# First linear attention's keys-times-values with values as weights in two column halves; four transferred tiles a head; logarithms and additions on other engines

## The reference

```python
# layer 0, "mix": a performer with 12 heads of 64, M = 384 features
q, k = _feature_map(q, w_orf), _feature_map(k, w_orf)   # exp(x w - |x|^2/2) / sqrt(M)
k_sum = jnp.sum(k, axis=2)
D = jnp.einsum('bhnm,bhm->bhn', q, k_sum)[..., None] + EPSILON
ktv = jnp.einsum('bhnm,bhnc->bhmc', k, v)
out = jnp.einsum('bhnm,bhmc->bhnc', q, ktv) / D
h = x + out @ proj_w + proj_b
y = _layernorm(h, ln2_g, ln2_b)
y = jax.nn.gelu(y @ fc1_w + fc1_b) @ fc2_w + fc2_b
# both layers, "gnn": graph attention with 8 heads
e = jax.nn.leaky_relu(a_src[src] + a_dst[dst], NEG_SLOPE)
ex = jnp.exp(e - m[dst])                 # m: largest e of a target
denom = jax.ops.segment_sum(ex, dst)
out = jax.ops.segment_sum(ex / denom[dst] * h[src], dst)
```

## Time and profile before

| quantity | us |
|---|---|
| median of 3 runs (3369.91 to 3375.5) | 3371.8 |
| the profiled execution | 3377.93 |
| its span | 3376.1 |
| PE busy | 2862.6 (85%) |
| DVE busy | 2279.2 (68%) |
| ACT busy | 1450.8 (43%) |
| POOL busy | 612.2 (18%) |

### The profile page before, as it was taken

One profiled execution on the slowest core, in us unless ns is written; L12 is line 12 of the kernel. 1 busy time (PEld: TensorE's weight loads), 2 busy tenths in 40 slices (PEclk: granted clock), 3 DMA queues, 4 the chain that ended last, 5 costly groups with the idle time before them and its releaser, 6 DMA issues. The chain is left out here.

```text
span 3376.1 us, 50914 instructions
## 1 busy us (share of the span) xinstructions
PE 2862.6 (85%) x17896; PEld 2539.2 (75%) x17896; DVE 2279.2 (68%) x4129; ACT 1450.8 (43%) x2440; POOL 612.2 (18%) x460
## 2 busy tenths in 40 slices
PE   4999997867999997798897599868999976998794
PEld 3999995666788997798896233248999976887794
DVE  6575543856851553798664888756797868998775
ACT  5465462222112332465243577621455532554355
POOL 2777782220000000110002310000000014110000
PEclk9999998988999999899999699979999988998897
DMA  8433326694212653976031312244302058864301
GB/s 272 82 47 57 55 15 171 196 231 109 69 46 68 188 168 99 214 143 143 30 76 33 96 39 47 51 146 131 92 26 67 23 147 216 182 138 108 81 16 48
DMA packets 262710, 351.49 MB, mean 104 GB/s; under 512 B 100252, under 2 KB 178589, under 8 KB 262366
## 3 DMA queue, kind: packets, MB, share of 16 engines
q1 hardware_dynamic: 176574, 272.11, 30.0%
q0 software_dynamic: 85920, 76.71, 11.8%
HBM read 266.35 MB, written 81.40 MB: 103 GB/s over the span
## 5 line engine op out<-in xcount | busy, mean ns | idle before, releaser
L213 POOL DMA_INDIRECT adj_d<-edge_val,edge_off x160 | 336.2, 2101 | 108.5 <-DMA adj_d<-edge_val,edge_off 48.1
L3340 DVE TENSOR_TENSOR expert_wgel<-expert_gel,expert_wps 128x417 f32<-128x417 f32 (+1 forms) x384 | 202.5, 584 | 55.3 <-PE expert_wps L3265 53.3
L2251 PE MATMUL gat00att_ops<-gat00att_h,gat00att_p 125*125 x1600 | 191.2, 284 | 46.6 <-ACT gat00att_p L2161 27.4
L2251 PEld LDWEIGHTS gat00att_ops<-gat00att_h,gat00att_p 125*125 125x125 f32 x1600 | 188.2, 197 | 49.7 <-issue 49.7
L2251 PE MATMUL gat10att_ops<-gat10att_h,gat10att_p 125*125 x1600 | 189.5, 283 | 37.5 <-ACT gat10att_p L2161 21.1
L3312 ACT ACTIVATE expert_gel<-expert_hps 128x417 f32<-128x417 f32 (+1 forms) x384 | 192.9, 519 | 56.2 <-DVE expert_wgel L3340 46.3
L2251 PEld LDWEIGHTS gat10att_ops<-gat10att_h,gat10att_p 125*125 125x125 f32 x1600 | 186.4, 198 | 40.7 <-issue 40.6
L737 ACT ACTIVATE xn_room<-perf_wide,perf_lnm 125x384 f32<-125x384 f32 (+2 forms) x228 | 114.2, 621 | 162.5 <-PE perf_wide L623 89.3
L599 PE MATMUL perf_wide<-y_lo,perf_qk_hi 128*128 128x416 f32 (+1 forms) x432 | 155.0, 359 | 21.5 <-DVE perf_qk_lo L783 21.4
L1361 PE MATMUL fc_ps<-y_lo,fc_w_hi 128*128 128x512 f32 (+1 forms) x432 | 155.1, 359 | 20.4 <-DVE fc_w_lo L1403 20.4
L1514 PE MATMUL fc_ops<-fc_w_hi,fc_x_lo 128*125 128x384 f32 x480 | 163.2, 340 | 7.1 <-DVE fc_w_lo L1566 7.1
(11 more groups left out here) (514 smaller groups left out, 8328.4 us busy)
## 6 DMA issues: line engine op xcount, KB each, us to landing
fc_w<-in_L_mix_fc_w SPq DMA_DIRECT2D x96, 384.0 KB
gat00att_e<-logs_d POOLq DMA_DIRECT2D x24, 546.9 KB, 6.9
gat10att_e<-logs_d POOLq DMA_DIRECT2D x24, 546.9 KB, 7.2
adj_d<-edge_zero POOLq DMA_DIRECT2D x22, 546.9 KB, 14.6
gat00proj_adj<-adj_d POOLq DMA_DIRECT2D x20, 546.9 KB, 8.3
edge_keys<-keys_d SPq DMA_DIRECT2D x20, 437.5 KB
gat00att_sh<-shift_d SPq DMA_DIRECT2D x16, 546.9 KB
sh<-shift_d SPq DMA_DIRECT2D x16, 546.9 KB
```

The source lines that it names most:

```text
L213: edges.nc.gpsimd.indirect_dma_start(out=edges.adj_flat[u].rearrange("(n a) -> n a", a=1), out_offset=bass.IndirectOffsetOnAxis(ap=edges.o ...
L2251: ins = pe.matmul(ops[0:TP, u, b, t * w:(t + 1) * w], p[:, s, (t0 + t) * TP:(t0 + t + 1) * TP], h[:, s, bass.ds(hd, 1), :], start=(s == 0 ...
L3340: dve.tensor_tensor(wgel[:, q % W, 0:cn], gel[:, q % 3, 0:cn], wps[:, q % 3, 0:cn], ALU.mult).then_inc(wgel_done, 1)
```

## The change

- LOGGED becomes (1, 3, 5, 7): four tiles a head in place of three get their logarithm by transfer. PE and ACT both go through the tiles in `order`.
- The logarithms are made in fc1 from the stored counts, no longer in gat00proj; there they were three, here four.
- gat00proj stores the mask strips between the stores of h.
- POOL's first clear in the norm stage waits for the third of five loads of x.
- In performer 0 (`folded=True`), k_t_v has v (125 x 64) as weights and kphi (384 columns) as moving operand; the even token tiles go to partitions 0 to 63 of the result, the odd to 64 to 127. DVE sums the keys over tokens, and PE adds the two halves and turns them by six small matmuls. The copy of ktv for the first head stands behind the split of v's weights and one count. Performer 1 is as before.
- proj_stage has no POOL work: DVE adds bias and row, and ACT normalises.

```diff
@@ -39,7 +39,7 @@
 EG = 4
-LOGGED = (1, 4, 7)
+LOGGED = (1, 3, 5, 7)
 PLAIN = tuple(t for t in range(NT) if t not in LOGGED)
@@ -277,7 +277,7 @@
                 pool.wait_ge(zeroed, 1)
-                pool.wait_ge(x_ld[pairs - 1], 32)
+                pool.wait_ge(x_ld[2], 32)
                 edges.clear(pool, edges.adj_flat[0:1])
@@ -457,6 +457,11 @@
         ktv = S.sb("ktv", [128, 2, mb_n, vw])
+        if folded:
+            halves, fold, ones = S.sb("halves", [128, m]), S.sb("fold", [128, HD]), S.sb("ones", [TP, 1])
+            ksum = edges.zero[:, 0:m] if edges is not None else S.sb("ksum", [TP, m])
+            halves_done, halves_kept, ksum_done, fold_set = (S.sem(s) for s in (
+                "halves_done", "halves_kept", "ksum_done", "fold_set"))
         den = S.sb("den", [TP, NT])
@@ -464,6 +469,7 @@
         o_ps = S.ps("o_ps", [128, 2, 512])
+        ktv_out = o_ps[:, 1, 256:256 + mb_n * vw] if folded else ktv_ps[:, 0:mb_n * vw]
         w_ld, w_high, w_split, o_st = S.sem("w_ld"), S.sem("w_high"), S.sem("w_split"), S.sem("o_st")
@@ -615,6 +621,8 @@
                         for n in range(n_k):
+                            if x == 1 and n == n_k - 3:
+                                fold_halves(0)
                             bank = feature_bank(K0[x] + n)
@@ -629,6 +637,8 @@
                                 pe.wait_ge(s_done, g * 6 + 3 + c + 3)
+                            if x == 1 and c == 1:
+                                fold_halves(1)
                             for mb in range(mb_n):
@@ -641,12 +651,33 @@
                         pe.wait_ge(v_done, i * 5 + 5)
+                        if folded:
+                            pe.wait_ge(halves_kept, g * 2 + x + 1)
+                            for t in range(NT):
+                                r = 64 * (t % 2)
+                                ins = pe.matmul(ktv_ps[r:r + 64, 0:m], v[:, t, 2 * u + x, 0:HD], kphi[:, t, :],
+                                                start=(t < 2), stop=(t >= NT - 2), tile_position=(0, r), skip_group_check=True)
+                            ins.then_inc(halves_done, 1)
+                            return
                         pe.wait_ge(ktv_kept, g * 2 + x + 1)
...
                                                 start=(t == 0), stop=(t == NT - 1))
+                        ins.then_inc(ktv_done, 1)
+
+                    def fold_halves(x):
+                        if not folded:
+                            return
+                        pe.wait_ge(ktv_kept, g * 2 + x + 1)
+                        pe.wait_ge(halves_kept, g * 2 + x + 2)
+                        pe.wait_ge(ksum_done, g * 2 + x + 2)
+                        for mb in range(mb_n):
+                            pe.matmul(ktv_out[:, mb * vw:mb * vw + HD], halves[:, mb * 128:(mb + 1) * 128], fold[:],
+                                      start=True, stop=True)
+                            ins = pe.matmul(ktv_out[:, mb * vw + HD:(mb + 1) * vw], ksum[:, mb * 128:(mb + 1) * 128], ones[:],
+                                            start=True, stop=True)
                         ins.then_inc(ktv_done, 1)
@@ -738,7 +771,11 @@
-                        act.wait_ge(ktv_done, g * 2 + x + 1)
+                        if folded:
+                            act.wait_ge(halves_done, g * 2 + x + 1)
+                            act.wait_ge(ksum_done, g * 2 + x + 1)
+                        else:
+                            act.wait_ge(ktv_done, g * 2 + x + 1)
                         for n in range(n_k):
@@ -850,9 +887,22 @@
+                    def sum_keys(x):
+                        if not folded:
+                            return
+                        dve.wait_ge(exp_done, g * units + K0[x] + n_k + 1)
+                        dve.wait_ge(ktv_done, g * 2 + x + 1)
+                        dve.tensor_reduce(ksum[:], kphi[:].rearrange("p t m -> p m t"), AX.X, ALU.add).then_inc(ksum_done, 1)
+
+                    def keep_halves(x):
+                        if not folded:
+                            return
+                        dve.wait_ge(halves_done, g * 2 + x + 2)
+                        dve.tensor_copy(halves[:], ktv_ps[:, 0:m]).then_inc(halves_kept, 1)
+
                     def keep_ktv(x):
                         dve.wait_ge(ktv_done, g * 2 + x + 2)
-                        dve.tensor_copy(ktv[:, x], ktv_ps[:, 0:mb_n * vw].rearrange("p (a b) -> p a b", a=mb_n)
+                        dve.tensor_copy(ktv[:, x], ktv_out.rearrange("p (a b) -> p a b", a=mb_n)
                                         ).then_inc(ktv_kept, 1)
@@ -885,15 +935,22 @@
                         scan.tiles(dve, hd, 0, 0, 2)
-                    keep_ktv(0)
+                    sum_keys(0)
+                    keep_halves(0)
+                    if not folded:
+                        keep_ktv(0)
                     if u == 0 and not (isinstance(i, int) and i == HP // 2 - 1):
...
                     count(1)
+                    if folded:
+                        keep_ktv(0)
+                    sum_keys(1)
                     keep_out(0)
                     count(2)
+                    keep_halves(1)
                     keep_ktv(1)
@@ -1165,6 +1230,11 @@
+                def normalise(t):
+                    act.wait_ge(centred, t + 1)
+                    act.activation(a[:, t, :] if turn else h[:, t, :], h[:, t, :], ACT.Identity, scale=rstd[:, t:t + 1],
+                                   bias=centre[:, t:t + 1]).then_inc(normed, 1)
+
                 def keep_a(t):
```

proj_stage on DVE, fc1, gat00proj and attention (`mask_after` is `{5: (0, 5), 8: (5, 9), 9: (9, 10)}`):

```diff
@@ -1262,25 +1312,25 @@
-                def normalise(t):
-                    if turn:
-                        if t in first_of:
-                            dve.wait_ge(x_ld[first_of[t]], 32)
-                        dve.tensor_tensor(x[:, t, :], x[:, t, :], h[:, t, :], ALU.add).then_inc(sum_ready, 1)
-
+                def scales(t):
                     dve.wait_ge(std_ready, t + 1)
...
                     steps_done.wait()
-                    dst = a[:, t, :] if turn else h[:, t, :]
-                    dve.tensor_scalar(dst, h[:, t, :], mv[:, t, 0:1], rstd[:, t:t + 1],
-                                      ALU.subtract, ALU.mult).then_inc(normed, 1)
-                    if not turn:
+                    dve.scalar_tensor_tensor(out=centre[:, t:t + 1], in0=mv[:, t, 0:1], scalar=-1.0, in1=rstd[:, t:t + 1],
+                                             op0=ALU.mult, op1=ALU.mult).then_inc(centred, 1)
+
+                def total(t):
+                    if t in first_of:
+                        dve.wait_ge(x_ld[first_of[t]], 32)
+                    if turn:
+                        dve.tensor_tensor(x[:, t, :], x[:, t, :], h[:, t, :], ALU.add).then_inc(sum_ready, 1)
+                    else:
+                        steps_done.done(dve.tensor_tensor(x[:, t, :], x[:, t, :], rows[0:TP, 1, :], ALU.add))
                         dve.wait_ge(normed, t + 1)
                         steps_done.done(dve.tensor_tensor(h[:, t, :], h[:, t, :], rows[0:TP, 0, :], ALU.mult))
-                        dve.wait_ge(shifted, t + 1)
                         steps_done.wait()
-                        total = late.tiles[:, t - NT + 2, :] if late is not None and t >= NT - 2 else x[:, t, :]
-                        dve.tensor_tensor(total, x[:, t, :], h[:, t, :], ALU.add).then_inc(sum_ready, 1)
+                        to = late.tiles[:, t - NT + 2, :] if late is not None and t >= NT - 2 else x[:, t, :]
+                        dve.tensor_tensor(to, x[:, t, :], h[:, t, :], ALU.add).then_inc(sum_ready, 1)
@@ -1343,10 +1404,19 @@
                 sp.wait_ge(next_st, 16)
+                sp.wait_ge(log_st, 32 * len(LOGGED))
...
                 scan.load(pool)
+                for n, s in enumerate(LOGGED):
+                    if n:
+                        pool.wait_ge(log_ready, n)
+                        move_rows(pool, logs_d[n - 1], log[:], log_st)
+                    move_rows(pool, counts[:], counts_d[s * TP:(s + 1) * TP, :], counts_ld)
+                pool.wait_ge(log_ready, len(LOGGED))
+                move_rows(pool, logs_d[len(LOGGED) - 1], log[:], log_st)
+                pool.wait_ge(log_st, 32 * len(LOGGED))
@@ -1389,10 +1459,13 @@
                 act.wait_ge(scan.scanned, 8)
-                with act.Fori(SB // 2 - 1, ob_n // 2 - 1) as i:
+                for i in range(SB // 2 - 1, ob_n // 2 - 1):
                     for u in range(2):
...
                         gelu(i * 2 + u + 1, 1 - u)
+                    n = i - SB // 2 + 1
+                    act.wait_ge(at_least_one, n + 1)
+                    act.activation(log[:], log[:], ACT.Ln).then_inc(logged, 1)
                 gelu(ob_n - 1, 1)
@@ -1420,9 +1493,18 @@
                         scan.finish(dve, hd, x)
-                with dve.Fori(SB // 2, ob_n // 2) as i:
-                    for u in range(2):
-                        low(i * 2 + u, u)
+                for i in range(SB // 2, ob_n // 2):
+                    n = i - SB // 2
```

(44 more changed lines are left out.)

94 lines of the change are left out of this document (45 added, 49 removed).

## The result

The changed kernel takes 3363.1 us (median of 13 runs) where the kernel before takes 3375.2 beside it: ratio 0.996, with an interval of 0.9945 to 0.9976. So it is faster by 12 us, not by 38, and lies 1 us above the range given, 3310 to 3362. (The forecast was made from a median of 3371.8 for before, 3.4 us under the one of all 13 runs.) Its profiled execution has a span of 3358.1 us, 18.0 less than that of before.

What follows compares the result with a forecast made beforehand. Read stage by stage, with PE's instructions setting performer 0's length. Gains 11 + 18 + 8.5 + 0 + 1 + 0 = 38.5 us took 3377.9 to 3339.4, or 3333 us against the median; own range 3318 to 3350, overall 3310 to 3362.

Steps and rivals of the forecast that it cites:

- The step that failed: Performer 0: DVE's key sums take 49 us in all; PE waits 1.6 us in two pairs, about 0.6 us a pair.
- the bound of 4.6 us: Performer 0: upper bound for one DVE key sum of 3840 elements, in proportion to 1.22 us for 1024.
- the first rival: Performer 0: column halves don't overlap, so it loses 25 us instead of gaining 11; 3369 us, chance 0.08.
- the loss at the change of mode: Performer 0: skill page's caution that changing tiling mode drains PE; trace leaves at most about 0.2 us, 24 changes.
- The scatter as next limit: Performer 0: POOL's scatter-adds end at 515.1 us, so the stage ends at 519.5, not 513.6; gain 11 us.
- gat00proj's total: gat00proj: 10.5 us from logarithms leaving plus 9.5 from the tail, less 2 for overlap; gain 18 us.
- the bound of 8: proj1: upper bound of the gain from moving POOL's additions to DVE, forecast at 4 us, lower bound -4.
- The earlier clear: Norm stage: first clear of the adjacency starts some 7 us earlier; gain 1 us, between -1.5 and 4.
- zero was forecast: Both attention stages: fourth transfer's 0.3 us a head offset by 2.4 us a stage at the start; bounds 10 either way.
- the second rival: Attention: accumulates run one behind another, 29.2 us a head for 25.15, 65 us lost; 3398 us, chance 0.08.
- The Trainium skill's formula: Attention: one transfer costs 2.0 us plus bytes at 436 GB/s, 3.3 us for 547 KB; 22 us more gain.
- DVE's new 23.7 a head: Attention: DVE's time per head in us with four transfers, set beside 24.1 us of DMA.

Runs made afterwards that it cites:

- The first run without the fold: Changed kernel with performer 0 as before (30 matmuls a head, no key sum on DVE), all other parts kept: ratio 0.9898, 3345.6 us.
- the short sum: Changed kernel with performer 0's key sum over two of ten token tiles, so denominators are not the reference's: ratio 0.9861, performer 0 471 us.
- the last reordering: Kernel with three transferred tiles and nine additions per key sum, DVE's sum moved ahead of query/key weight split and first count: ratio 0.983, 3322.6 us.
- the two runs on order and number: Performer 0 as before: three transferred tiles with PE in ACT's order, attention 0 234.8 us; four with PE from 0 to 9, 243.1 us.

## Why the prediction was wrong

**The step that failed** is the sum on DVE and what it does to PE: "12 x 4.1 = 49 us on an engine with 262 of 469 us busy", and behind it "PE comes to the fold early: I estimate 1.6 us there, and about 0.6 us a pair". The sum is 6.8 us, 81 in all. It was scaled from a reduction of 1024 neighbouring elements to one of 3840 in another shape, and the bound of 4.6 us taken from it was no bound. (With 0.1 us of each fixed the scaled value is 4.3, not 4.1; 4.1 needs 0.17.) Then it is not so that "ACT's wait for the sum ends before its wait for PE's features": ACT waited 22.5 us in five times for the sum, and PE's matmuls at L630 8.8 us in four times for ACT, where before they waited there for DVE's operands alone. The first run without the fold showed that 26 us go with it, the short sum that the sum is their source, and the last reordering that the place of the work in DVE's queue counts as much as its size: 19 us.

**What the prediction did not have at all** is the clock. It priced a stall by its length. PE's clock in performer 0 was 0.97 before; in after the four new waits of 2.0 to 3.8 us were each followed by 7 to 20 us at 0.50. That is 33 of the 28 + 24 = 52 us that were lost, and filling two waits of 1.4 us with useless matmuls gave 14 us back. The rows of before hold a warning, though a small one: there the wait of 2.56 us in the middle of a head's key features made that group 8.0 us, and 3.8 + 2.5 is 6.3. A price of 1.7 us a wait, taken from it, would still have been far under the 5 to 8 us measured.

**Right:** the matmuls (3.5 forecast, 3.45 measured) and the fold (1.4 and 1.39), so the first rival fell, and with it the loss at the change of mode: the 3.45 us include it. The scatter as next limit: not reached in the changed kernel, reached at 520.8 + 3.9 in the one with the sum first. But it is no fixed limit: with the same instructions of POOL it ended between 503 and 525 us in the kernels here. gat00proj's total (18 and 18.7), though by about 13.0 + 5.5 and not 10.5 + 9.5 less 2 for overlap: two misses that cancel. proj0 (4.5 and 4.7); no addition of DVE there is stretched, each takes 0.91 to 0.96 us. fc1, at zero, cost 1.6 us by its profile (in before it ends at 1072.0, not 1071).

**Too small:** proj1 gave 9.4 us, above the bound of 8, though DMA went from 0.89 to 0.95. DVE's stretching went about as counted, and its busy time only from 79.3 to 76.5 us; but before, DVE also waited 7.3 us in four times for POOL's addition to h, and that is gone. How much of the 9.4 us it is was not tried. The earlier clear gave 5.3 and not 1, above its bound of 4.

**Attention:** zero was forecast, 7.6 us were lost by the two profiles, inside the bounds; the other kernels bear out the loss of attention 0 alone. In attention 0 DVE has 11.6 us less to do, but waited 8 us more for the first loads, where 2.4 were forecast, and 5.5 for ACT's p. The loss is at the start: from PE's first matmul of one head to that of the next, the first two heads took 75.8 us for 68.5 before, the other six 147.8 for 150.5, 24.6 each for 25.1. (In the two runs on order and number the last six do not part this way.) Single ones of these six took up to 27.0 us before and 27.3 after, so the prediction's sign for the second rival, one head at 27 us, could not tell; the mean can, and it fell. The transfers overlap (median landing 7.3 before, 8.0 after). (The prediction's "DVE's new 23.7 a head" should be 24.55 - 1.45 = 23.1; nothing rests on it.)

The Trainium skill's formula ("DMA: Bandwidth & Descriptors", section "Anatomy of one DMA — SWDGE (gpsimd) path") would have put the time 22 us lower still, further off than the row; the landings measured here are 5.4 to 13.3 us, for the 3.3 us estimated from that page.

The sum without performer 0 was 38.5 - 11 = 27.5 us. The changed stages other than it gave 5.3 + 18.7 + 4.7 - 2.7 - 4.3 + 9.4 - 3.3 = 27.8 us. That these agree is luck: norm and proj1 are together 9.7 us over their forecast, attention and fc1 with fc2 10.3 under it. Beside these, the unchanged stages gave about 17. With performer 0 at its measured +28, and those, the 18 us of the two profiles come out.

## What to carry to other kernels

A microsecond that PE waits in a full stretch can have a second price, the time at half clock behind it: here between nothing and 8 us of work for a wait of 1.4 to 2.6 us. Look for rows of the same kernel in which PE has waited, compare the group behind the wait with its like, and take the spread as a bound, not one row as the price.

When work moves from a full engine to one with free time, look at what stands in that engine's queue at the moment the result is wanted, not at its share. Here two orders of the same work in the queue differed by 19 us, most of the 24 us that the new matmuls had saved on PE.

Put a result of some microseconds beside the stages that were not changed before calling it the change's, and look at the "instruction" packets of loops in them.
